# A four-layer graph network on one core: the residuals of layer 3's bf16 parts move from GpSimd to VectorE, one copy on ScalarE is dropped, and every engine's order is written anew

## The chip, the core and the metric

The program runs on one core of a Trainium2 chip. The metric is the device time of one execution in microseconds. Its five engines run queues of their own and meet at semaphores: TensorE (PE), VectorE (DVE), ScalarE (ACT), GpSimd (POOL) and SyncE (SP), which issues all DMAs.

## The reference

`x` and `adj` are 128 graphs of 128 nodes with 128 features. Four layers follow each other, each with a residual and a layer norm:

```python
x = layernorm(x + L0(x, adj, adj, ...))   # attention, 8 heads, edge bias, masked softmax, output projection
x = layernorm(x + L1(x, adj, ...))        # convolution of 17 taps, message passing with exp(-dist), gated unit
x = layernorm(x + L2(x, adj, ...))        # additive attention, softmax of e_i + f_j with mask
x = layernorm(x + L3(x, adj, ...))        # graph attention, 4 heads
# in L3:
e = e_i[:, :, :, None] + e_j[:, :, None, :]
e = where(e > 0, e, 0.2 * e); e = where(adj > 0, e, -9e15)
out = softmax(e) @ h
```

The change sits in L3's logits. Their sum `e_i + e_j` is a matmul of bf16 operands. Each fp32 number goes in as three bf16 parts: the rounded value, the rounded rest, and the rest of that.

## The kernel before, in words

Graphs go in 32 groups of four (`GB = 4`); a tile `[128, 512]` holds a group. All four layers of different groups are in flight together. Each engine has a function `step(t)` that lists its operations in an order written out by hand, each with the group it works on (`t - 38` and so on), and a loop runs it for all `t`. Operations whose group is out of range do nothing, so at the start only layer 0 runs and at the end only layer 3. The constant in `t - 38` matters only beside the others of the same engine: every engine runs its own stream.

PSUM has eight banks, `B[0]` to `B[7]`, and nearly every result of PE passes one. An operation that takes a bank first calls `freed(engine, s, users)`, which waits for the last live user in the list handed to it. So the order of an engine, the bank of each result and these lists belong together.

On PE (L839 to L976) the scores of layer 0 come in two halves (`scores`, L540), on slices of 32 rows of the array, `values` (L562), `targets` (L792), `values3` (L819) and `embed` (L664) on slices of 32 columns, `logits3` (L801) and `distances` (L683) again on rows. The rest uses the whole array. Helpers: every transposition is recorded at L508, the convolution's products at L605, the gates' matmuls at L708.

On DVE `seed_edges` (L1368) writes the edge bias into a bank before the scores add to it, and `seed_mask3` (L1603) does it for layer 3. `row_max` (L1382) and `row_max3` (L1611) take the negated row maxima, on which the exponentials on ACT, `exps` (L1011) and `exps3` (L1169), wait. ACT also copies nearly all banks to SBUF (`keep_...`), applies `leaky` (L1162), and makes the squares (L1069) that `sides` (L1440) on DVE needs for the distances. Copies of the transposed probabilities are L1028 (layer 0) and L1186 (layer 3). POOL takes the differences for the convolution (`fir_first`, L383, writes `xs`; `fir_second`, L397, writes `xd` and `xf`), multiplies `aT` by the mask (L413) and computes 1/sqrt by pow (L370).

The bf16 parts arise like this. `targets` puts e_i and e_j, repeated on several partitions, into the first 128 columns of `B[2]`. `keep_ej` (L1154) on ACT copies them to `ej` in fp32 (L1159) and to `ejh` in bf16 (L1160). `split_ej` (L415) on POOL subtracts: `ejt`, `ejv`, `ejd`, `eju`, `ejw` (L424 to L432), where a factor `neg_s` of 0 or -1 on each partition says which part this partition holds. Then four instructions L435 and one L436 make `ejm` and `eim`, the operands of `logits3`, by a factor and an addend on each partition.

SP (L305) loads the group's inputs: `xt` into two buffers, `xn` into two, `at` into three, `an` into six, and stores the result.

## Time and profile before

| what | value |
|---|---|
| median of 3 runs | 1408.46 us (1406.12 to 1408.89) |
| the profiled execution | 1408.24 us |
| its span, from the first instruction to the last | 1406.5 us |
| mean granted TensorE clock | 0.98 |
| PE, DVE, ACT, POOL busy | 96%, 86%, 84%, 42% |
| matmul instructions | 13330 |
| HBM traffic | 31 GB/s |

The span is the stretch that the profile's rows cover; the execution's own time has 1.7 us around it. A busy engine is one with an instruction under way: for PE, whose matmuls overlap, the record of a matmul reaches beyond the start of the next, so the starts tell more than the durations. In the tables a row ends with the idle time of the engine before it and what ended that.

### The profile page before, as it was taken

The numbers are of one execution on the slowest core, as the hardware profiler recorded it, in microseconds if no ns is written. First come the engines' busy times: TensorE is split into PE (matmuls) and PEld (weight loads), VectorE is DVE, ScalarE is ACT, GpSimd is POOL, SyncE is SP. The second block draws the span as 40 slices with busy tenths as digits, with TensorE's granted clock in tenths as the row PEclk, the third lists the DMA queues.
The fourth block names the chain that finished last, engine by engine and source line by source line (L and its number), as shares of the span: only waits on it lengthen the run. The fifth ranks groups of instructions, "written<-read, shape, count | busy, mean of one in ns | idle before, by whom it ended". The sixth has DMA issues, their size and how long they took to land.

```text
span 1406.5 us, 40636 instructions
## 1 busy us (share of the span) xinstructions
PE 1344.6 (96%) x13330; PEld 1043.0 (74%) x13330; DVE 1212.4 (86%) x3407; ACT 1185.0 (84%) x4450; POOL 596.5 (42%) x918
## 2 busy tenths in 40 slices
PE   6799999999999999999999999999999999999974
PEld 3577778877777877777787777787777778777753
DVE  7658889889999988999888999989898999888874
ACT  6877888988888998888898888889888888986664
POOL 1123444544344444435344434445443444545532
PEclk8999999999999999999999999999999999999995
DMA  3101010001011011101101101110110111000000
GB/s 134 31 31 32 31 32 31 17 32 39 16 40 39 25 38 39 32 24 39 39 24 39 40 17 38 39 39 24 39 39 17 39 39 32 24 17 31 9 16 24
DMA packets 23826, 46.88 MB, mean 33 GB/s; under 512 B 2753, under 2 KB 2754, under 8 KB 23490
## 3 DMA queue, kind: packets, MB, share of 16 engines
q1 hardware_dynamic: 23618, 44.27, 10.0%
q8 instruction: 110, 1.80, 0.5%
q14 instruction: 98, 0.80, 0.2%
HBM read 35.88 MB, written 8.39 MB: 31 GB/s over the span
## 4 chain that ended last, share of the span: by engine, by line
PE 89%; ACT 4%; DVE 4%; issue 2%; POOL 1%; DVEq 0%; POOLq 0%; ACTq 0%
PE B L708 18%; PE B L605 17%; PE B L508 14%; PE B L548 5%; PE B L572 4%; PE B L618 3%; PE B L519 2%; PE B L534 2%; PE B L761 2%; PE B L789 2%; PE B L662 2%; PE B L702 2%; PE B L827 2%; PE B L595 2%; PE B L773 2%; PE B L679 2%
## 5 line engine op out<-in xcount | busy, mean ns | idle before, releaser
L1019 ACT ACTIVATE e<-B,nm 128x128 f32<-128x128 f32 x1024 | 362.7, 384 | 12.8 <-DVE nm L1387 12.8
L508 PE MATMUL B<-ident,e 128*128 128x128 f32 x1536 | 233.5, 279 | 17.2 <-ACT pT L1028 8.8
L1377 DVE SCALAR_TENSOR_TENSOR B<-an,rowb,mask 128x512 f32<-128x512 f32 x256 | 190.6, 789 | 50.9 <-ACT h L1152 42.2
L1019 ACT ACTIVATION_READ_ACCUMULATOR e<-B,nm 128x1 f32 x1024 | 231.0, 226 | 0.0
L508 PEld LDWEIGHTS B<-ident,e 128*128 128x128 f32 x1536 | 178.8, 143 | 35.9 <-issue 12.3
L1177 ACT ACTIVATE e<-l,nm 128x128 f32<-128x128 f32 x512 | 198.7, 402 | 5.5 <-DVE nm L1616 5.5
L377 POOL TENSOR_TENSOR veps<-meanv,eps 128x4 f32<-128x4 f32 x128 | 26.4, 206 | 399.6 <-DVE meanv L1350 399.6
L1387 DVE TENSOR_REDUCE nm<-B 128x4 f32<-128x512 f32 x256 | 168.7, 673 | 26.2 <-PE B L548 26.0
L1028 ACT ACTIVATE pT<-B 128x512 f32<-128x512 f32 x256 | 155.6, 620 | 1.7 <-PE B L508 1.7
L380 POOL TENSOR_TENSOR rstd<-veps,neghalf 128x4 f32<-128x4 f32 x128 | 130.0, 1016 | 10.0
L391 POOL TENSOR_TENSOR xs<-xs 128x288 f32<-128x288 f32 x32 | 40.8, 1276 | 203.6 <-ACT xs L1059 203.6
L708 PE MATMUL B<-x1T,wm 128*128 128x512 f32 x192 | 102.4, 615 | 0.9 <-ACT nmT L1099 0.4
L1177 ACT ACTIVATION_READ_ACCUMULATOR e<-l,nm 128x1 f32 x512 | 103.0, 201 | 0.0
L548 PEld LDWEIGHTS B<-kh,qT 32*128 32x128 f32 x2048 | 63.8, 188 | 50.6 <-issue 47.9
L708 PE MATMUL B<-xcT,wm 128*128 128x512 f32 x192 | 98.2, 593 | 0.0
L708 PE MATMUL B<-nmT,wm 128*128 128x512 f32 x192 | 98.0, 592 | 0.0
L1115 ACT ACTIVATE tr<-B,gb 128x512 f32<-128x512 f32 x32 | 22.0, 687 | 88.0 <-PE B L708 88.0
L1616 DVE TENSOR_REDUCE nm<-l 128x4 f32<-128x512 f32 x128 | 86.9, 679 | 9.7 <-ACT l L1167 9.3
L605 PE MATMUL B<-xd,wm 128*128 128x128 f32 x640 | 90.5, 279 | 3.0 <-DVE B L1481 3.0
L1608 DVE TENSOR_SCALAR B<-an 128x512 f32<-128x512 f32 x128 | 81.8, 686 | 12.9 <-ACT pT L1028 12.9
L1167 ACT ACTIVATE l<-B 128x512 f32<-128x512 f32 x128 | 72.8, 594 | 23.2 <-PE B L809 22.1
L1186 ACT ACTIVATE pT<-B 128x512 f32<-128x512 f32 x128 | 76.8, 600 | 17.3 <-PE B L508 16.3
(200 smaller groups left out, 3423.5 us busy)
## 6 DMA issues: line engine op xcount, KB each, us to landing
xt<-in_x_t SPq DMA_DIRECT2D x32, 256.0 KB, 3.4
an<-in_adj_n SPq DMA_DIRECT2D x32, 256.0 KB, 2.9
xn<-in_x_n SPq DMA_DIRECT2D x32, 256.0 KB, 3.0
at<-in_adj_t SPq DMA_DIRECT2D x32, 256.0 KB, 2.7
out_x<-xo SPq DMA_DIRECT2D x32, 256.0 KB, 3.3
wm<-in_mats SPq DMA_DIRECT2D x1, 1088.0 KB, 9.1
wm<-in_mats SPq DMA_DIRECT2D x1, 832.0 KB, 6.7
wm<-in_mats SPq DMA_DIRECT2D x1, 320.0 KB, 2.9
```

The lines of the kernel that those rows point to most:

```text
L380: pool.tensor_tensor(rstd[i][:, :], veps[i][:, :], neghalf[:, :], ALU.pow)\
L508: last = mm(g(dst, b), g(src, b), ident[:, :], is_transpose=True, start=(b == 0), stop=True, skip_group_check=True)
L548: last = mm(g(banks[j], b), qT[r, b * N:(b + 1) * N], kh[r, e, b * N:(b + 1) * N], start=False, stop=True, skip_group_check=True)
L605: last = mm(phases(bank[:, :])[:, slot], w, src[:, :, c:c + Q], start=(start and c == 0), stop=True, skip_group_check=True)
L708: last = mm(bank[:, :], wm[:, w + j * N:w + (j + 1) * N], src[:, :], start=(n == 0 and not onto), stop=(n == len(parts) - 1), skip_group_c ...
L1019: last = fn(g(e0[:, h % 2, :], b), g(bank, b), ACT.Exp, bias=nm0[:, h % 4, b:b + 1], accum_out=sum0[s % 2][:, b, head(h):head(h) + 1])
L1028: fn(pT0[:, h, :], bank[:, :], ACT.Copy).then_inc(q["pT_ready"], 1)
L1177: last = fn(g(e3[:, b % 2, :], h), g(l3[:, b % 2, :], h), ACT.Exp, bias=nm3[:, b % 2, h:h + 1], accum_out=sum3[s % 2][:, b, h:h + 1])
L1377: v.scalar_tensor_tensor(out=bank[:, :], in0=an[s % AN][:, :], scalar=we[:, head(h):head(h) + 1], in1=mask0[:, :], op0=ALU.mult, op1=ALU.a ...
L1387: v.tensor_reduce(nm0[:, h % 4, :], per(bank[:, :]), AX, ALU.max, negate=True).then_inc(q["nm_ready"], 1)
L1608: v.tensor_scalar(per(bank[:, :]), g(an[s % AN], b).unsqueeze(1).broadcast_to([128, H3, N]), 0.0, NEG3, ALU.is_le, ALU.mult).then_inc(q["s ...
L1616: v.tensor_reduce(nm3[:, b % 2, :], per(l3[:, b % 2, :]), AX, ALU.max, negate=True)\
```

## The change

`keep_ej` makes one copy, `ejh`, and waits for the `ejw` of the group before. A new function `residuals3` on DVE makes `ejv`, `ejd` and `ejw` in three instructions, the first of which reads the bank itself. `split_ej` keeps the last five instructions. The prologue's bank for small products is `B[0]` in place of `B[5]`. The order on all five engines is new, and with it many banks and all lists for `freed`. Every engine but SP has its groups shifted by five more steps.

```diff
-ROWS, SMALL = 3, 5
+ROWS, SMALL = 3, 0
...
-STEPS = GROUPS + 46
+STEPS = GROUPS + 51
...
             def step(t):
+                store(t - 9)
+                load_xn(t - 2)
+                load_at(t - 4)
+                load_an(t)
                 load_xt(t)
-                load_at(t - 2)
-                load_an(t)
-                load_xn(t)
-                store(t - 10)
...
                 wait(pool, q["e3_ps"], GB * s)
-                pool.wait_ge(q["ej_ready"], s + 1)
-                pool.tensor_scalar(ejt[:, :], ejh[:, :], neg_s[:, 0:1], 1.0, ALU.mult, ALU.mult).then_inc(q["ej_t1"], 1)
-                pool.wait_ge(q["ej_t1"], s + 1)
-                pool.tensor_tensor(ejv[:, :], ejt[:, :], ej[:, :], ALU.add).then_inc(q["ej_v"], 1)
-                pool.wait_ge(q["ej_v"], s + 1)
-                pool.tensor_scalar(ejd[:, :], ejv[:, :], 1.0, 1.0, ALU.mult, ALU.mult).then_inc(q["ej_d"], 1)
-                pool.wait_ge(q["ej_d"], s + 1)
-                pool.tensor_scalar(eju[:, :], ejd[:, :], neg_s[:, 1:2], 1.0, ALU.mult, ALU.mult).then_inc(q["ej_t2"], 1)
-                pool.wait_ge(q["ej_t2"], s + 1)
-                pool.tensor_tensor(ejw[:, :], eju[:, :], ejv[:, :], ALU.add).then_inc(q["ej_w"], 1)
                 pool.wait_ge(q["ej_w"], s + 1)
...
-                rsqrt(1, t - 43)
-                rsqrt(3, t - 46)
...
+                rsqrt(3, t - 51)
+                rsqrt(1, t - 48)
...
             def keep_ej(s, bank):
...
-                wait(act, q["ej_split"], s)
+                wait(act, q["ej_w"], s)
                 act.wait_ge(q["ej_ps"], s + 1)
-                fn(ej[:, :], bank[:, 0:N], ACT.Copy)
                 fn(ejh[:, :], bank[:, 0:N], ACT.Copy).then_inc(q["ej_ready"], 1)
...
+            def residuals3(s, bank):
+
+                if not live(s):
+                    return
+                wait(dve, q["ej_split"], s)
+                dve.wait_ge(q["ej_ready"], s + 1)
+                v.scalar_tensor_tensor(out=ejv[:, :], in0=ejh[:, :], scalar=neg_s[:, 0:1], in1=bank[:, 0:N],
+                                       op0=ALU.mult, op1=ALU.add).then_inc(q["ej_v"], 1)
+                dve.wait_ge(q["ej_v"], s + 1)
+                v.tensor_copy(ejd[:, :], ejv[:, :]).then_inc(q["ej_d"], 1)
+                dve.wait_ge(q["ej_d"], s + 1)
+                v.scalar_tensor_tensor(out=ejw[:, :], in0=ejd[:, :], scalar=neg_s[:, 1:2], in1=ejv[:, :],
+                                       op0=ALU.mult, op1=ALU.add).then_inc(q["ej_w"], 1)
```

The new orders, from the added lines of the three long `step` functions (the lists for `freed` and some calls are left out; the removed lines are the orders of the kernel before). PE:

```diff
+                gate_r(t - 46, B[3], (("n3_done", -3, 1, 1), ("em_ready", 0, 1, 1), ("kh1_ready", 3, 1, 1),
...
+                scores(t - 43, 0, (B[6], B[4], B[1], B[2]))
+                gate_z(t - 46, B[0], (("r2_done", -1, 1, 1), ("pT3_ready", -2, 4, 1),
...
+                sums_T(t - 44, B[3], (("tr_ready", -2, 1, 1), ("n3_done", -5, 1, 1),
...
+                probs3_T(t - 48, 1, B[7], (("r2_done", 1, 1, 1), ("qT_ready", 5, 1, 1),
...
+                values(t - 44, 0, B[5], (("pT_ready", 0, 8, 8), ("em_ready", -2, 1, 1),
...
+                values(t - 44, 1, B[5], ())
+                gate_hn(t - 46, B[3], (("recT_ready", 2, 1, 1), ("tr_ready", 0, 1, 1),
...
+                probs_T(t - 43, 0, B[7], (("pT3_ready", -5, 4, 2), ("r2_done", -4, 1, 1),
...
+                x1_T(t - 45, B[4], (("exp_done", 2, 8, 2), ("l3_done", -3, 4, 4), ("exp_done", 1, 8, 7),
...
+                hidden3(t - 48, B[6], (("exp_done", 5, 8, 1), ("xc_ready", 2, 1, 1), ("l3_done", 0, 4, 2),
...
+                probs_T(t - 43, 1, B[5], (("oT_ready", -1, 1, 1), ("pT_ready", -1, 8, 8),
...
+                gate_in(t - 46, B[0])
+                project_v(t - 43, B[7], (("pT_ready", 0, 8, 1), ("pT3_ready", -5, 4, 2),
...
+                probs_T(t - 43, 2, B[1], (("exp_done", 0, 8, 3), ("ln_out1", -4, 1, 1),
...
+                scores(t - 43, 1, (B[3], B[6], B[4], B[5]))
+                conv1(t - 45, B[1], (("pT_ready", 2, 8, 3), ("exp_done", 2, 8, 3), ("ln_out1", -2, 1, 1),
...
+                x3_T(t - 47, B[2], (("exp_done", 4, 8, 4), ("nmT_ready", 1, 1, 1), ("em_ready", 1, 1, 1),
...
+                probs3_T(t - 48, 2, B[0], (("n_ready", 2, 1, 1), ("tz_ready", 2, 1, 1),
...
+                project_out(t - 44, B[7], (("v_ready", 1, 1, 1), ("pT_ready", 1, 8, 1),
...
+                probs3_T(t - 48, 3, B[1], (("hp_ready", 3, 1, 1), ("pT_ready", 5, 8, 3),
...
+                targets(t - 47, B[2], (("x3T_ready", 0, 1, 1), ("exp_done", 4, 8, 4),
...
+                probs_T(t - 43, 3, B[0], (("pT3_ready", -5, 4, 3), ("n_ready", -3, 1, 1),
...
+                values3(t - 48, B[7], (("res0_done", 4, 1, 1), ("v_ready", 5, 1, 1), ("pT_ready", 5, 8, 1),
...
+                embed(t - 45, B[1], (("pT3_ready", -3, 4, 4), ("hp_ready", 0, 1, 1), ("pT_ready", 2, 8, 3),
...
+                logits3(t - 47, (B[3], B[6], B[0], B[4]))
+                probs_T(t - 43, 6, B[2], (("pT_ready", 0, 8, 6), ("v0_done", -2, 1, 1), ("ej_v", -4, 1, 1),
...
+                project_k(t - 42, B[3], (("l3_done", -5, 4, 1), ("exp_done", -1, 8, 5),
...
+                hidden2(t - 46, (B[2], B[5]), (("pT_ready", 3, 8, 7), ("pT_ready", 3, 8, 6),
...
+                conv_own(t - 45, 0, B[6])
+                distances(t - 45, (B[7], B[5], B[2], B[3]), (("v2_done", 0, 1, 1), ("o3T_ready", -3, 1, 1),
...
+                conv_own(t - 45, 1, B[6])
+                out3_T(t - 48, B[3], (("em_ready", 3, 1, 1), ("kh1_ready", 6, 1, 1), ("l3_done", 1, 4, 1),
...
+                project_q(t - 42, B[7], (("em_ready", -3, 1, 1), ("v2_done", -3, 1, 1),
...
+                probs3_T(t - 47, 0, B[0], (("l3_done", 0, 4, 3), ("pT_ready", 4, 8, 5),
...
+                gather(t - 45, B[2], (("em_ready", 0, 1, 1), ("hb_done", -1, 1, 1), ("pT_ready", 2, 8, 7),
...
+                numerators(t - 46, (B[0], B[7]), (("pT3_ready", -1, 4, 1), ("l3_done", -1, 4, 3),
...
```

ACT:

```diff
+                exps3(t - 49, 2)
+                tanh_r(t - 47, B[3])
+                keep_probs(t - 45, 7, B[5])
+                exps(t - 44, 0, B[6])
+                exps(t - 44, 1, B[4])
+                keep_sums(t - 45, B[3])
+                tanh_z(t - 47, B[0])
+                keep_probs3(t - 49, 1, B[7])
+                exps3(t - 49, 3)
+                exps(t - 44, 2, B[1])
+                keep_h3(t - 49, B[6])
+                keep_x1(t - 46, B[4])
+                keep_probs(t - 44, 0, B[7])
+                keep_probs(t - 44, 1, B[5])
+                exps(t - 44, 3, B[2])
+                keep_probs(t - 44, 2, B[1])
+                tanh_n(t - 47, B[0])
+                keep_v(t - 44, B[7])
+                conv_input(t - 46, B[1])
+                keep_x3(t - 48, B[2])
+                keep_probs3(t - 49, 2, B[0])
+                keep_probs3(t - 49, 3, B[1])
+                keep_ej(t - 48, B[2])
+                exps(t - 44, 4, B[3])
+                keep_out3(t - 49, B[7])
+                keep_d(t - 46, B[1])
+                keep_probs(t - 44, 3, B[0])
+                exps(t - 44, 5, B[6])
+                squares(t - 46)
+                exps(t - 44, 6, B[4])
+                keep_probs(t - 44, 4, B[0])
+                keep_probs(t - 44, 5, B[2])
+                exps(t - 44, 7, B[5])
+                message_relu(t - 46)
+                leaky(t - 48, 0, B[3])
+                leaky(t - 48, 1, B[6])
+                keep_probs(t - 44, 6, B[2])
+                exps3(t - 48, 0)
+                keep_k(t - 43, 0, B[3])
+                keep_k(t - 43, 1, B[3])
+                exp_edges(t - 47)
+                leaky(t - 48, 2, B[0])
+                affinity(t - 46, (B[7], B[5], B[2], B[3]))
+                exps3(t - 48, 1)
+                conv_relu(t - 46, B[6])
+                keep_q(t - 43, B[7])
+                keep_probs3(t - 48, 0, B[0])
+                leaky(t - 48, 3, B[4])
+                keep_gathered(t - 46, B[2])
```

DVE:

```diff
+                seed_edges(t - 43, 2, B[1], (("ln_out1", -4, 1, 1), ("m1_done", -3, 1, 1),
...
+                row_scales(t - 47, (B[0], B[7]))
+                seed_edges(t - 43, 3, B[2], (("nmT_ready", -3, 1, 1), ("em_ready", -3, 1, 1),
...
+                residual2(t - 47, (B[0], B[7]))
+                invert_sums(t - 44)
+                stats2(t - 47)
+                row_max(t - 43, 0, B[6])
+                row_max(t - 43, 1, B[4])
+                norm0(t - 45)
+                half_tanh(t - 46)
+                aggr2(t - 47)
...
+                divide(t - 44, B[5])
+                reset_hn(t - 46, B[3], B[0], (("tz_ready", 0, 1, 1), ("r2_done", -1, 1, 1),
...
+                seed_edges(t - 43, 4, B[3], (("g1_done", -3, 1, 1), ("recT_ready", -1, 1, 1),
...
+                seed_edges(t - 43, 5, B[6], (("h3_ready", -5, 1, 1), ("exp_done", 0, 8, 1),
...
+                seed_edges(t - 43, 6, B[4], (("x1T_ready", -2, 1, 1), ("exp_done", 0, 8, 2),
...
+                seed_edges(t - 43, 7, B[5], (("pT_ready", 0, 8, 2), ("oT_ready", -1, 1, 1),
...
+                norm2(t - 47)
+                stats3(t - 49)
+                z_times_n(t - 46)
+                row_max(t - 43, 4, B[3])
+                aggr3(t - 49)
+                gru_out(t - 46)
+                row_max(t - 43, 5, B[6])
+                residual0(t - 44, B[7])
+                residuals3(t - 47, B[2])
+                stats0(t - 44)
+                row_max(t - 43, 6, B[4])
+                seed_mask3(t - 47, 0, B[3], (("exp_done", 4, 8, 5), ("g1_done", 1, 1, 1),
...
+                shared_to_all(t - 45, B[2])
+                sides(t - 45)
+                message_bias(t - 45, B[1])
+                seed_mask3(t - 47, 1, B[6], (("exp_done", 4, 8, 6), ("h3_ready", -1, 1, 1),
...
+                row_max(t - 43, 7, B[5])
+                seed_mask3(t - 47, 2, B[0], (("pT_ready", 4, 8, 5), ("pT_ready", 4, 8, 4),
...
+                seed_mask3(t - 47, 3, B[4], (("exp_done", 4, 8, 7), ("x1T_ready", 2, 1, 1),
...
+                stats1(t - 46, B[1])
+                shared_to_phases(t - 45, B[7])
+                aggr1(t - 46)
+                row_max3(t - 47, 0)
+                shared_to_halves(t - 45, B[7], B[6], (("l3_done", -2, 4, 2), ("exp_done", 2, 8, 6),
...
+                invert_sums3(t - 48)
+                row_max3(t - 47, 1)
+                hidden_bias(t - 46, (B[2], B[5]))
+                edge_mask(t - 42)
+                norm3(t - 49)
+                hidden_times_e(t - 46)
+                norm1(t - 46, B[1])
+                row_max3(t - 47, 2)
+                seed_edges(t - 42, 0, B[6], (("xc_ready", -3, 1, 1), ("l3_done", -5, 4, 2),
...
+                aggr0(t - 44)
+                divide3(t - 48, B[3])
+                seed_edges(t - 42, 1, B[4], (("l3_done", -5, 4, 4), ("exp_done", -1, 8, 7),
...
```

## Rows read from the trace of the kernel before

**Rows 1.** The page: busy time of each engine, and the chain that ended last.

```profile
PE 1344.6 (96%) x13330; PEld 1043.0 (74%) x13330; DVE 1212.4 (86%) x3407; ACT 1185.0 (84%) x4450; POOL 596.5 (42%) x918
...
PE 89%; ACT 4%; DVE 4%; issue 2%; POOL 1%; DVEq 0%; POOLq 0%; ACTq 0%
```

**Rows 2.** Windows: us, PE, PEld, DVE, ACT, POOL busy, PE clock, DMA share, GB/s.

```profile
397.90:1141.40 743.50, 740.18 (x7488) 578.67 (x7488) 673.41 (x1892) 662.22 (x2503) 335.51 (x504) 1.00 0.11 34
...
1330.00:1406.50 76.50, 45.38 (x328) 33.16 (x326) 48.74 (x166) 41.21 (x143) 23.30 (x42) 0.73 0.05 18
```

**Rows 3.** Waits of PE, 397.9 to 1141.4 us: total, times, longest.

```profile
PE B L519 <- ACT l L1167: 3.2, 18, 0.2
```

**Rows 4.** Timeline of PE: start, us, engine, line, op, out<-in.

```profile
700.22 1.17 PE L548 MATMUL B<-kh,qT 32*128 32x128 f32 x32
...
727.19 0.39 PE L809 MATMUL B<-ejm,eim 32*128 32x512 bf16 x4
...
732.20 0.50 PE L692 MATMUL B<-lr,ll 32*128 32x128 f32 x8
```

**Rows 5.** Timeline of ACT, the same period.

```profile
719.14 0.33 ACT L1160 ACTIVATE ejh<-B 128x128 bf16<-128x128 f32 x1
719.63 0.60 ACT L1193 ACTIVATE o3T<-B 128x512 f32<-128x512 f32 x1 [0.16 <-PE B L827]
...
722.60 0.53 ACT L1075 ACTIVATE sqr<-dd,sel 128x128 f32<-128x128 f32 x1
...
727.70 1.09 ACT L1167 ACTIVATE l<-B 128x512 f32<-128x512 f32 x2 [0.28 <-PE B L809]
...
729.57 1.27 ACT L992 ACTIVATE kh<-B,parity 128x512 f32<-128x512 f32 x2 [0.30 <-PE B L519]
```

**Rows 6.** Timeline of POOL, the same period.

```profile
715.83 1.37 POOL L391 TENSOR_TENSOR xs<-xs 128x288 f32<-128x288 f32 x1 [6.60 <-ACT xs L1059]
...
720.85 0.36 POOL L424 TENSOR_SCALAR ejt<-ejh,neg_s 128x128 f32<-128x128 bf16 x1
...
723.26 1.87 POOL L435 TENSOR_SCALAR ejm<-ejw,mid_t,mid_i 128x128 bf16<-128x128 f32 x4
...
733.90 1.28 POOL L413 TENSOR_TENSOR aT<-aT,at 128x512 f32<-128x512 f32 x1 [2.75 <-ACT aT L1089]
```

**Rows 7.** Single lines of code: duration ns min/median/max, first and last start us.

```profile
L1580 DVE SCALAR_TENSOR_TENSOR r<-B,wr,x x128: 340/341/351, 123.9 to 1367.8; 128x128 f32<-128x128 f32 x128
...
L1554 DVE COPY hg<-eg x32: 165/1257/1269, 117.5 to 1363.7; 128x8 f32<-128x8 f32 x32
...
L1446 DVE SCALAR_TENSOR_TENSOR lr<-dd,sel,sqr x32: 334/438/454, 73.0 to 1327.9; 128x128 f32<-128x128 f32 x32
...
L1377 DVE SCALAR_TENSOR_TENSOR B<-an,rowb,mask x256: 742/753/1115, 7.0 to 1250.4; 128x512 f32<-128x512 f32 x128
...
L405 POOL TENSOR_TENSOR xf<-xs x32: 1083/1534/1567, 70.6 to 1324.2; 128x420 f32<-128x420 f32 x32
...
L391 POOL TENSOR_TENSOR xs<-xs x32: 792/1377/1381, 67.8 to 1321.0; 128x288 f32<-128x288 f32 x32
```

**Rows 8.** Timeline of DVE, the same period.

```profile
715.87 0.67 DVE L1505 TENSOR_TENSOR zn<-zminus,nT 128x512 f32<-128x512 f32 x1
...
717.97 0.69 DVE L1412 TENSOR_TENSOR r<-B,xn 128x512 f32<-128x512 f32 x1 [0.82 <-PE B L595]
718.58 0.68 DVE L1387 TENSOR_REDUCE nm<-B 128x4 f32<-128x512 f32 x1
...
733.95 1.26 DVE L1554 COPY hg<-eg 128x8 f32<-128x8 f32 x1
```

**Rows 9.** The chain that ended last, 1340 us to the end: start, us, what.

```profile
1352.58 0.28 ACT ej L1159
...
1355.62 1.09 POOL ejm L435 x3
...
1389.80 2.08 PE B L789 x8
```

More of the change, by code:

```diff
@@ L483, in _ @@
             pe.wait_ge(q["flat_set"], 1)
-            for i in (0, 1, 2):
+            for i in (1, 2, 4):
                 set_bank(i)
@@ L1195, in step @@
             def step(t):
-                conv_relu(t - 42, B[6])
-                keep_probs3(t - 44, 0, B[5])
-                keep_q(t - 39, B[0])
-                leaky(t - 44, 3, B[4])
-                keep_gathered(t - 42, B[2])
-                keep_probs(t - 40, 7, B[5])
-                tanh_r(t - 42, B[3])
-                exps3(t - 44, 2)
-                exps(t - 39, 0, B[6])
-                exps(t - 39, 1, B[4])
-                tanh_z(t - 42, B[0])
-                keep_sums(t - 40, B[3])
@@ L1221, in step @@
-                keep_x3(t - 43, B[2])
-                keep_probs3(t - 44, 3, B[7])
-                exps(t - 39, 4, B[6])
-                keep_ej(t - 43, B[2])
-                keep_out3(t - 44, B[7])
-                keep_d(t - 41, B[1])
-                keep_probs(t - 39, 3, B[0])
-                exps(t - 39, 5, B[3])
-                squares(t - 41)
-                exps(t - 39, 6, B[4])
-                keep_probs(t - 39, 4, B[0])
-                keep_probs(t - 39, 5, B[2])
-                exps(t - 39, 7, B[5])
@@ L1234, in step @@
-                message_relu(t - 41)
-                leaky(t - 43, 0, B[3])
-                leaky(t - 43, 1, B[6])
-                keep_probs(t - 39, 6, B[2])
-                keep_k(t - 38, 1, B[3])
-                keep_k(t - 38, 0, B[3])
-                exps3(t - 43, 0)
-                leaky(t - 43, 2, B[0])
-                exp_edges(t - 42)
-                affinity(t - 41, (B[3], B[7], B[5], B[2]))
-                exps3(t - 43, 1)
+                exps3(t - 49, 2)
+                tanh_r(t - 47, B[3])
@@ L1699, in step @@
-                stats1(t - 41, B[1])
-                shared_to_phases(t - 40, B[7])
-                aggr1(t - 41)
-                row_max3(t - 42, 0)
-                shared_to_halves(t - 40, B[7], B[6], (("l3_done", -2, 4, 2), ("exp_done", 2, 8, 5),
-                    ("exp_done", 2, 8, 1), ("xc_ready", -1, 1, 1)))
-                stats0(t - 39)
-                hidden_bias(t - 41, (B[2], B[5]))
-                row_max3(t - 42, 1)
-                norm3(t - 44)
-                hidden_times_e(t - 41)
```

338 lines of the change are left out of this document (120 added, 218 removed).

## The prediction

> **What bounds the kernel now.** I read the page first: the matmul engine is busy 96% of the span, and is 89% of the chain that ended last [rows 1]. Then the stages: of PE's 13330 matmuls each of the 32 groups has 416, so the 7488 between 397.9 and 1141.4 us are 18 groups [rows 1, 2], in 743.5 us at full clock, so 41.3 us a group, with PE busy for 740.2 of it; the last 76.5 us have PE busy for 45.4 only, at clock 0.73 [rows 2]. In the steady stretch PE waits by the profile for one thing, 0.2 us a group, at L519 [rows 3]. So in the middle a change pays only if it takes PE's small stalls away, and costs if it makes new ones; at the end PE waits for chains through the other engines. One executed period, 700.22 (scores) to 741.61, serves as my ruler [rows 4]; all clock times below are in it.
>
> The profiled execution took 1408.24 us, 1.7 over its span; the median is 1408.46, so the two stand for each other. A measurement here tells about 0.2%, 2.8 us, from no change.
>
> **Part by part: edits with one answer.** The banks are renamed; the set-up loop still sets seven; each engine keeps its instructions but for those below. PE loses and gains nothing. It alternates between whole-array matmuls and those on row or column slices; values0 and values1 become one block, targets leaves values3, so there are seven such blocks a group as before, and adding up PE's starts I get the instruction behind them as far from the scores as in the ruler, within 0.02 us. 0 us. SP: store, xn, at, an, xt in place of xt, at, an, xn, store. What the first load now stands behind is the layer 3 mask seeding of six groups earlier (for an), about 727 in the ruler; xt, the last of the five, is wanted by a project_k a period later. 0 us. POOL's rsqrt order: norm 3's statistics are ready long before, 0 us. Bank B2 is released by the first residual instead of the copy, still before conv_both wants it: 0 us.
>
> **The copy dropped.** ACT issues two copies 0.16 us apart and the second stays, at 719.14. Next on ACT stands the copy of values3, for which it waited 0.16 us [rows 5], so the gain goes into that wait: 0 us. But keep_ej moves ahead of exps 4: ready at 718.46 rather than 719.47.
>
> **The residuals.** POOL loses five instructions, 0.36 + 0.46 + 0.30 + 0.37 + 0.45 us, which with their handovers take 720.85 to 723.26 [rows 6]. That is off the path in the middle: the five masks behind them take 2.3 more, to 725.55, and logits3 starts at 727.19 [rows 4]. DVE gains three dependent instructions. First: one SBUF, one PSUM operand, 128x128; the nearest row is L1580, 0.34 [rows 7]. Second, an SBUF copy to bf16: between the 0.17 of the 8-element copy L1554 and L1580's 0.34 [rows 7]; I take 0.2, since the copy has one operand only. Third, two SBUF operands: L1446 at its least, 0.33 [rows 7]. With 0.05 between them, 1.0 us in all.
>
> But such operands have another price beside POOL. The copy L1554 takes 0.165 at least and 1.257 in the median; in the timeline it starts at 733.95, 0.05 after POOL's mask product, and ends with it [rows 6 to 8]. The two-operand seed L1377 takes 0.753 in the median and 1.115 where it meets a POOL instruction [rows 7]. L1580, one operand in PSUM, never lengthens. In the new order DVE reaches the residuals at 718.5, while POOL runs fir_second: conv_input ends about 0.65 later than now (conv1 stands behind scores1), so xd runs about 718.6 to 719.7 and xf, 1.08 at its least [rows 7], behind it. So the second residual waits for xd, 0.65 us, and the third for xf: from 0.35 (the seed's excess) to 1.09 (the copy's excess) [rows 7]; I take the middle, 0.7. The residuals end near 720.85 instead of 719.5. Bounds: 1.0 us to 2.75 us in all.
>
> The Trainium skill, "SBUF — State Buffer", Who interferes with whom, says that VectorE and GpSimd share one port pair as an exclusive lock, held for the whole instruction by whoever issues first. By that sentence taken literally the third residual would wait out all of xf (0.9 more than unhindered), and the sum would be 1419.3 in place of 1413.9. The trace agrees on the waiting but not on who wins: z_times_n started 0.04 after POOL's xs and ran its normal 0.67, while xs took 1.37 instead of its least, 0.79 [rows 6 to 8].
>
> **What waits for them.** Behind the residuals DVE has stats0 (0.78), row_max 6, seed_mask 0, shared_to_all (0.60 each, as the starts are apart [rows 8]): 720.85 + 2.58 = 723.4. Next is sides, which waits for ACT's second square, 723.13 as now [rows 5]. So of the cost only what passes 720.6 counts: 0.2 us. From there the chain has no gap: sides 0.71, then message_bias, mask 1, row_max 7, masks 2 and 3, 0.60 each, the last 0.69: 727.2, plus 0.07 to PE, against 727.19 [rows 4]. **Term 1: logits3 late by 0.1.** Row_max 7 ends at 726.0, now 721.4; behind it ACT has exps 7 (1.37) and message_relu (0.5), so leaky 0 can start at 727.9 and not at 727.70 [rows 5], and project_k waits for leaky 0 [rows 3]: **term 2: 0.12 more.** On DVE stats1, shared_to_phases, aggr1 (1.83) come before row_max3 0, which so ends at 729.6. ACT now has exps3 0 (1.53) ahead of both keep_k (1.27 [rows 5]): they end at 732.48. The distances need B3 from the second keep_k; in the ruler they start at 732.20 [rows 4], with 0.22 of delay at 732.42. **Term 3: 0.12 with the handover.** Sum 0.34 us a group. Layer 3 runs together with layer 1 in 27 of the periods: **+9.2 us**.
>
> Now for what the new order spares. Gate_hn in B3, residual2 before the row maxima, exps3 2 before tanh_r, for which ACT stood idle: each fills a wait of an engine that isn't the bound, 0 us. The copy L1554 may now slip ahead of POOL's product and save DVE 1.09 us; after it nothing of PE's waits on DVE until the seeds, 0 us.
>
> **The end.** Twice, for groups 30 and 31, the residuals are on the chain: ej at 1352.58, ejm at 1355.62 [rows 9], 3.04 us, and the same again 23 us later. DVE is free and POOL idle there, so the three take 0.33 + 0.07 + 1.0 + 0.15 = 1.55: 1.45 saved, twice 2.9. At 1389.80 hidden3 has waited for the copy of pT3 [rows 9], since both use B3; in B6 it goes about 2 us earlier, then transposition 3 waits for exps3 3 near 1391.3: 0.9 saved. At the start, scores1 waits for keep_probs 1 (seed 7 uses its bank) and exps 4 comes some 0.1 later in three groups: +0.3. **-3.5 us**.
>
> Sum: 1408.24 + 9.2 - 3.5 = **1413.9 us**, 0.4% slower. Own range of this case 1411.5 to 1418.
>
> **Rivals.** (a) Faster: POOL does not hold DVE up, or the residuals end before 720.6. For: DVE stands 0.8 us idle at residual0 [rows 8], so there is slack. Then terms 1 and 2 vanish, and if row_max3 0 ends by 729.3 also term 3: 1408.24 - 3.5 = 1404.7. Chance 0.23. (b) No change: the residuals hide, but keep_k behind exps3 0 does not: 0.14 a group (row_max3 0 ends at 729.45 at best by my chain), 27 x 0.14 = 3.8, 1408.5. Chance 0.20. (c) Slower still: the third residual waits for the whole of xf, 0.2 more; terms 0.29, 0.12, 0.13, together 0.54: 1404.7 + 14.6 = 1419.3. The port rule of the Trainium skill gives this one. It decides from 720.6 on; every 0.1 us later costs 2.7 us. Against: xs above. Chance 0.20. (d) That SP's new order starves a load: excluded by the slack above, under 0.01.
>
> The forecast has 0.37. So slower 0.57, same 0.20, faster 0.23. Range 1403 to 1424: below, case (a) with its small stalls; above, (c) with 0.17 a group more, as my sums along queues may be off by 0.2.
>
> **What would show it.** The new copy near 0.8 us instead of 0.2 and the last residual near 1.0 instead of 0.34 in the middle, both short in the last two groups; PE waits at logits3 and the distances that rows 3 do not have; a period of 41.6 to 41.7 us; project_k's wait longer; the last 76 us shorter by 3. It is wrong if the period stays at 41.3 or less, or if sides still has DVE waiting for the squares.

## The result, and the profile after

| | before | after |
|---|---|---|
| median | 1408.89 us (7 runs, 1406.12 to 1411.19) | 1413.09 us (7 runs, 1412.05 to 1414.99) |
| the profiled execution, its span | 1408.24, 1406.5 | 1413.09, 1411.4 |

The ratio is 1.0032, 95% interval 1.0022 to 1.0042: 0.3% slower, where 1413.9 was forecast. The total came out closer than its parts did, which is luck, as the account of the parts below shows.

The page after: busy time of each engine, and the chain that ended last.

```profile
PE 1348.3 (96%) x13330; PEld 1048.3 (74%) x13330; DVE 1238.0 (88%) x3503; ACT 1182.6 (84%) x4418; POOL 509.0 (36%) x758
...
PE 69%; DVE 14%; ACT 10%; issue 5%; POOL 1%; DVEq 0%; ACTq 0%; POOLq 0%
```

Beside [rows 1]: POOL is busy for 87.5 us less and DVE for 26 more, 0.8 us for each of the 32 groups. That is less than the residuals take (2.2 us a group in the middle, below), above all because the copy L1538 (L1554 before) has become short, 0.164 us in the median instead of 1.257. ACT has 32 copies fewer. The bound is PE as before, but the chain now runs over DVE and ACT for 24% instead of 8% of the span.

Windows: us, PE, PEld, DVE, ACT, POOL busy, PE clock, DMA share, GB/s.

```profile
397.90:1141.40 743.50, 736.96 (x7456) 577.33 (x7455) 683.87 (x1937) 658.08 (x2468) 279.45 (x408) 1.00 0.11 34
1330.00:1411.40 81.40, 51.69 (x422) 39.63 (x422) 57.68 (x185) 43.72 (x148) 24.79 (x41) 0.79 0.05 17
```

The same 743.5 us hold 32 matmuls fewer than in [rows 2], and PE is busy for 3.2 us less. From project_k to project_k, over 18 groups, the period is 41.514 us against 41.306 before.

Waits of PE after, 397.9 to 1141.4 us: total, times, longest.

```profile
PE B L506 <- ACT l L1151: 4.4, 18, 0.5
PE B L679 <- issue: 1.0, 4, 0.2
```

The first is project_k's wait of [rows 3], 1.2 us more. The second is at the distances, and small only because most of that wait lies under the modelled length of the matmul before. PE's starts tell more. I added up the steps from each start to the next over the 18 groups, by what follows what. Mean per group, after less before: from the convolution to the distances +0.171 (0.384 against 0.214); around y_T +0.060 (nothing before); from the transposition to project_k +0.067; from gather to the embedding behind it -0.08; the rest -0.01. Sum +0.21.

The timelines show the new residuals and what stands around them. DVE, then POOL, ACT and PE of one period after: start, us, engine, line, op, out<-in, [idle before <- what ended it].

```profile
765.30 0.35 DVE L1593 SCALAR_TENSOR_TENSOR ejv<-ejh,neg_s,B 128x128 f32<-128x128 bf16 x1 [0.57 <-ACT ejh L1144]
765.68 0.84 DVE L1596 CAST ejd<-ejv 128x128 bf16<-128x128 f32 x1
766.57 1.07 DVE L1598 SCALAR_TENSOR_TENSOR ejw<-ejd,neg_s,ejv 128x128 f32<-128x128 bf16 x1
...
769.52 0.68 DVE L1442 TENSOR_TENSOR vT<-B,x1T 128x512 f32<-128x512 f32 x1
770.13 0.35 DVE L1430 SCALAR_TENSOR_TENSOR lr<-dd,sel,sqr 128x128 f32<-128x128 f32 x1
770.40 0.35 DVE L1432 SCALAR_TENSOR_TENSOR ll<-dd,sel,sql 128x128 f32<-128x128 f32 x1
770.66 0.68 DVE L1421 TENSOR_TENSOR msg<-B,rowb 128x512 f32<-128x512 f32 x1
```

```profile
765.33 1.11 POOL L401 TENSOR_TENSOR xd<-xs 128x432 f32<-128x432 f32 x1
766.41 1.08 POOL L402 TENSOR_TENSOR xf<-xs 128x420 f32<-128x420 f32 x1
767.82 1.75 POOL L422 TENSOR_SCALAR ejm<-ejw,mid_t,mid_i 128x128 bf16<-128x128 f32 x4 [0.33 <-DVE ejw L1598]
```

```profile
769.43 0.57 ACT L1060 ACTIVATE sqr<-dd,sel 128x128 f32<-128x128 f32 x1
```

```profile
771.44 0.62 PE L495 MATMUL B<-ident,yT 128*128 128x128 f32 x4
...
774.00 0.39 PE L796 MATMUL B<-ejm,eim 32*128 32x512 bf16 x4
```

The first residual is short beside POOL's xd. The second ends 0.08 us after xd, the third 0.15 after xf. They take 2.3 us where 1.0 would do. But sides (L1430) starts 0.13 us behind ACT's square, so most of that was hidden.

How closely the two arrive is told by the start of sides beside the end of shared_to_all (L1442) ahead of it: where nothing holds DVE up, the next instruction starts before the recorded end of the last (sides 0.09 us before it in the kernel before, in the median of the 18 groups), here 0.01 behind it. So DVE stood about 0.1 us for the squares. Behind sides stands message_bias (L1421, ends at 771.34), and 0.10 later PE starts y_T, which waits for it.

So there are two accounts of the slower middle: the stretch of the residuals (the forecast), or the orders, namely a chain without slack through ACT's squares to y_T, and exps3 0 ahead of keep_k. The experiments are to tell them apart.

Periods in them are means over 18 groups from PE's starts. The ratios are to the kernel before, run beside each of the three sets (medians 1410.10, 1408.79 and 1408.84 us). The changed kernel was timed with the result only, so differences from its 1413.09 us compare different sets, and those of a microsecond or two rest on the periods and not on the times.

### The profile page after: what moved, and what is told of

Same layout as the page of the kernel before. It is cut to its first block, busy times and chain, and to the rows that moved or that the text cites. A ratio compares the mean times of both kernels' runs of the same rounds, so it can differ in the third digit from the quotient of the medians.

```text
span 1411.4 us, 40570 instructions
## 1 busy us (share of the span) xinstructions
PE 1348.3 (96%) x13330; PEld 1048.3 (74%) x13330; DVE 1238.0 (88%) x3503; ACT 1182.6 (84%) x4418; POOL 509.0 (36%) x758
## 4 chain that ended last, share of the span: by engine, by line
PE 69%; DVE 14%; ACT 10%; issue 5%; POOL 1%; DVEq 0%; ACTq 0%; POOLq 0%
PE B L695 18%; PE B L495 11%; PE B L592 10%; PE B L535 5%; ACT e L1004 5%; PE B L559 4%; DVE nm L1371 3%; DVE B L1606 3%; PE B L506 2%; PE B L649 2%; PE B L760 2%; PE B L521 2%; PE B L748 2%; PE B L689 2%; PE B L513 2%
## 5 line engine op out<-in xcount | busy, mean ns | idle before, releaser
L1004 ACT ACTIVATE e<-B,nm 128x128 f32<-128x128 f32 x1024 | 367.8, 398 | 46.5 <-DVE nm L1371 39.6
L495 PE MATMUL B<-ident,e 128*128 128x128 f32 x1536 | 241.1, 281 | 21.8 <-ACT pT L1013 6.5
L1004 ACT ACTIVATION_READ_ACCUMULATOR e<-B,nm 128x1 f32 x1024 | 242.8, 237 | 0.0
L495 PEld LDWEIGHTS B<-ident,e 128*128 128x128 f32 x1536 | 183.2, 144 | 72.0 <-issue 50.0
L374 POOL TENSOR_TENSOR veps<-meanv,eps 128x4 f32<-128x4 f32 x128 | 34.9, 272 | 342.7 <-DVE meanv L1334 342.7
L1013 ACT ACTIVATE pT<-B 128x512 f32<-128x512 f32 x256 | 151.9, 632 | 3.0 <-PE B L495 2.2
L388 POOL TENSOR_TENSOR xs<-xs 128x288 f32<-128x288 f32 x32 | 30.9, 965 | 231.5 <-ACT xs L1044 231.5
L1161 ACT ACTIVATION_READ_ACCUMULATOR e<-l,nm 128x1 f32 x512 | 109.5, 214 | 0.0
L1170 ACT ACTIVATE pT<-B 128x512 f32<-128x512 f32 x128 | 77.5, 607 | 15.9 <-PE B L495 15.8
L410 POOL TENSOR_TENSOR aT<-aT,at 128x512 f32<-128x512 f32 x32 | 40.8, 1276 | 127.3 <-ACT aT L1074 127.3
L592 PEld LDWEIGHTS B<-xd,wm 128*128 128x128 f32 x640 | 78.8, 189 | 8.0 <-issue 4.1
```

The source lines that it names most:

```text
L495: last = mm(g(dst, b), g(src, b), ident[:, :], is_transpose=True, start=(b == 0), stop=True, skip_group_check=True)
L592: last = mm(phases(bank[:, :])[:, slot], w, src[:, :, c:c + Q], start=(start and c == 0), stop=True, skip_group_check=True)
L1004: last = fn(g(e0[:, h % 2, :], b), g(bank, b), ACT.Exp, bias=nm0[:, h % 4, b:b + 1], accum_out=sum0[s % 2][:, b, head(h):head(h) + 1])
L1013: fn(pT0[:, h, :], bank[:, :], ACT.Copy).then_inc(q["pT_ready"], 1)
L1161: last = fn(g(e3[:, b % 2, :], h), g(l3[:, b % 2, :], h), ACT.Exp, bias=nm3[:, b % 2, h:h + 1], accum_out=sum3[s % 2][:, b, h:h + 1])
```

## The experiments

**1. Four kernels: the residuals back, keep_k back, the residuals moved, the residuals alone.** a_pool takes the residual part of the change back in the new orders:

```diff
+                fn(ej[:, :], bank[:, 0:N], ACT.Copy)
                 fn(ejh[:, :], bank[:, 0:N], ACT.Copy).then_inc(q["ej_ready"], 1)
...
-                residuals3(t - 47, B[2])
```

> The changed kernel with the residuals back on GpSimd and both copies back on ScalarE; all other orders as changed. Theory 1 (the forecast: the stretched residuals on VectorE are what delays logits3, project_k and the distances): VectorE loses 2.2 us a group, the period falls from 41.51 to about 41.30 us, 27 x 0.21 = -5.7 us, and the end loses the 1.45 us of the last group: about 1409 us. Theory 2 (the stretch hides, because `sides` behind it waits for ScalarE's squares anyway; the distances wait because exps3 0 now stands ahead of keep_k): nothing is gained in the middle, and the second copy puts the squares up to 0.16 us later: period 41.5 to 41.7 us, 1414.5 to 1419 us.

Measured: 1422.26 us, 1.0088 (1.0074 to 1.0102), period 41.752. That is above both theories. Taking the residuals off DVE made the kernel slower by 9 us and not faster by 4, which speaks against their stretch as the main cost; but the second copy came back with them, and a_copy below separates the two. PE waits 0.17 us more at y_T and 0.10 more behind gather. The period's 0.238 us make some 6 of the 9 us (27 x 0.238); group 6 started 2.1 us later than in the changed kernel's profile.

a_keepk:

```diff
-                exps3(t - 48, 0)
                 keep_k(t - 43, 0, B[3])
                 keep_k(t - 43, 1, B[3])
+                exps3(t - 48, 0)
```

> The changed kernel with keep_k 0 and 1 ahead of exps3 0 on ScalarE, as before the change; nothing else. Theory 2 (queue order on ScalarE): the two copies end 1.5 us earlier, PE's step from convolution to distances falls from 0.38 to about 0.21 us, the period from 41.51 to 41.34, 27 x 0.17 = -4.6: 1408.5 us. Rival: exps3 0 ends 1.25 us later, and the transposition of its result or leaky 2 behind it holds PE up instead: 1412 us or more.

Measured: 1408.62 us, 0.9991 (0.9982 to 1.0000), 4.5 us less than the changed kernel. The period is 41.319, and PE's step to the distances 0.213 us, as before the change. ACT's timeline after, where the copies (L977) stand behind four exps3 without a gap and end at 737.54, and PE's, which starts the distances 1.13 us after the convolution's last block:

```profile
734.74 0.40 ACT L1161 ACTIVATE e<-l,nm 128x128 f32<-128x128 f32 x1
...
736.30 1.24 ACT L977 ACTIVATE kh<-B,parity 128x512 f32<-128x512 f32 x2
```

```profile
736.66 1.05 PE L592 MATMUL B<-xf,wm 128*128 128x128 f32 x8
737.79 0.45 PE L679 MATMUL B<-lr,ll 32*128 32x128 f32 x5
```

and the same two places in a_keepk, 0.98 us from the one to the other:

```profile
734.49 1.26 ACT L977 ACTIVATE kh<-B,parity 128x512 f32<-128x512 f32 x2 [0.30 <-PE B L506]
```

```profile
736.13 1.05 PE L592 MATMUL B<-xf,wm 128*128 128x128 f32 x8
737.11 0.50 PE L679 MATMUL B<-lr,ll 32*128 32x128 f32 x8
```

a_split cuts residuals3 in two (the first instruction stays) and calls the rest later on DVE:

```diff
                 seed_mask3(t - 47, 0, B[3], (("exp_done", 4, 8, 5), ("g1_done", 1, 1, 1),
...
+                residuals3_rest(t - 47)
                 shared_to_all(t - 45, B[2])
```

> The changed kernel with the second and third residual moved on VectorE behind stats0, row_max 6 and seed_mask 0, where GpSimd has finished xf; the first stays. Both theories expect them to take 0.23 and 0.35 us instead of 0.76 and 1.07. Theory 1 (the stretch is the cost): -0.2 us a group or a little more, 1407 to 1408 us. Theory 2 (`sides` waits for the squares anyway and starts at most 0.1 us earlier): 0 to -2 us, 1411 to 1413 us.

Measured: 1417.19 us, 1.0046 (1.0033 to 1.0059), period 41.594. Both theories missed: it is 4 us slower than the changed kernel. The period accounts for 2.2 of them (27 x 0.080); in the profile group 6 started 2.5 us later (196.5 instead of 194.0), which is within what starts of the same instructions differ by (below). The residuals are short, but DVE gains nothing by it:

```profile
770.96 0.22 DVE L1600 CAST ejd<-ejv 128x128 bf16<-128x128 f32 x1
771.21 0.35 DVE L1602 SCALAR_TENSOR_TENSOR ejw<-ejd,neg_s,ejv 128x128 f32<-128x128 bf16 x1
...
773.54 0.51 DVE L1430 SCALAR_TENSOR_TENSOR lr<-dd,sel,sqr 128x128 f32<-128x128 f32 x1 [1.38 <-ACT sqr L1060]
```

DVE stands idle for 1.38 us until the squares: the whole stretch was hidden there. And sides now meets POOL's ejm and eim (771.74 to 773.91), which puts 0.14 us on lr (0.509 in the median instead of 0.370); PE's step at y_T grew by 0.11. So the same wait came back in the one place that has no slack.

b_dve is the kernel before with this alone:

```diff
-                fn(ej[:, :], bank[:, 0:N], ACT.Copy)
...
                 row_max(t - 38, 7, B[5])
+                residuals3(t - 42, B[2])
```

> The kernel before with one part of the change alone: one copy on ScalarE, and the three residuals on VectorE, put behind row_max 7, where GpSimd has finished xf. All orders stay as before. Both theories: the residuals are short (0.35, 0.23, 0.35 us), the 1.0 us is taken up by VectorE's idle time ahead of the third mask, the period stays at 41.30, and the end is 1.45 us shorter once or twice: 1405.5 to 1407.5 us against 1408.9. Rival (a busy VectorE passes 1 us on): 0.3 to 0.5 us a group, 1416 to 1420 us.

Measured: 1495.44 us, 1.0605 (1.0591 to 1.0620), period 44.359. That is 88 us above what both theories expected, for a reason that neither had. Waits of PE in b_dve, 397.9 to 1141.4 us:

```profile
PE B L608 <- DVE ejv L1598: 34.2, 17, 2.8
```

The first residual reads bank 2 and so frees it, and conv_both behind it on PE waits for it, 2 us a group. The period grew by 3.05. The third microsecond lies behind the wait: in the period of the ruler PE stands idle for 1.96 us up to 721.48, and its granted clock, 1.00 before, is 0.76 from 721.5 to 723.5 and 0.50 (the lower of its two levels, 1.2 GHz) from 723.5 to 725.5 us, where the eight matmuls of message take 1.92 us. Behind row_max 7 is too late for the first residual: here the bank sets how late it can stand.

**2. Four more: the y_T chain, the start, the residuals alone again, the port.** a_swap:

```diff
+                message_bias(t - 45, B[1])
                 sides(t - 45)
-                message_bias(t - 45, B[1])
```

> The changed kernel with message_bias ahead of sides on VectorE; nothing else. From the four runs before: y_T (transposition of layer 2's input, bank 1) waits for message_bias, and that stands behind sides, which waits for ScalarE's squares. Theory 2 (this chain, not the stretched residuals, is VectorE's part of the price): PE's step before y_T falls by the 0.06 us that it has too much, the rest of VectorE's queue ends when it did, 41.51 to 41.45 us, 27 x 0.06 = -1.6: 1411.5 us. Theory 1 (the residuals' stretch): with nothing waiting for the squares, VectorE's whole queue is a chain from the residuals to row_max 7, and the distances' wait stays: 0 to -0.5 us.

Measured: 1409.82 us, 1.0006 (0.9997 to 1.0015), period 41.398. The 0.060 us at y_T are gone, with 0.030 at the distances and 0.022 at project_k: 0.117 us a group, twice what was expected, and 3.3 us less than the changed kernel, for one line.

a_fill:

```diff
+FIRST = 4
...
-                project_v(t - 43, B[7], (("pT_ready", 0, 8, 1), ("pT3_ready", -5, 4, 2),
...
+                if t - 43 >= FIRST:
+                    project_v(t - 43, B[7], (("pT_ready", 0, 8, 1), ("pT3_ready", -5, 4, 2),
...
                 scores(t - 43, 1, (B[3], B[6], B[4], B[5]))
+                if t - 43 < FIRST:
+                    project_v(t - 43, B[7], (("pT_ready", 0, 8, 1), ("pT3_ready", -5, 4, 2),
```

> The changed kernel in which PE issues project_v of the first four groups behind scores 1, as the kernel before does, and of all others where the change put it. Theory: PE's 2.1 us of project_v at half clock ahead of scores 1 of group 0 are what made the start 2.2 to 2.5 us longer: project_k of group 1 starts at 28.2 to 29 instead of 30.4 us, and the time falls by 2 us: 1411 us. Rival: the start is set by ScalarE's exponentials and VectorE's preparation, and the order on PE matters for group 0 alone or not: 0 to -0.5 us.

Measured: 1433.88 us, 1.0179 (1.0162 to 1.0196). The kernel was not what its expectation says: `FIRST` is set again further down in it, to 640 (`FIRST, SECOND = N * 5, WC2`), so project_v stood behind scores 1 for all groups, and the test of the start is spoilt for the total. What it shows: in the middle scores 1 then wait for DVE's seeds, which project_v had covered (period 42.035, 0.59 us a group at that step). At the start scores 1 came 1.9 us earlier (19.4 instead of 21.3 us), but project_k of group 1 still began at 30.8 us (30.4 in the changed kernel), so this place alone does not explain the longer start.

b_dve2 is b_dve with keep_ej ahead of exps 4, the first residual behind residual0 and the other two behind row_max 7:

```diff
+                keep_ej(t - 43, B[2])
                 exps(t - 39, 4, B[6])
-                keep_ej(t - 43, B[2])
...
                 residual0(t - 39, B[1])
+                residuals3(t - 42, B[2])
...
                 row_max(t - 38, 7, B[5])
+                residuals3_rest(t - 42)
```

> The kernel before with keep_ej (one copy) ahead of exps 4, the first residual behind residual0 on VectorE, so that bank 2 is free at 719.6 in the ruler and the convolution, 719.7, does not wait as it did in b_dve, and the other two behind row_max 7. All other orders as before. Theory 2: period 41.30 to 41.35 and the end 1.45 to 2.9 us shorter: 1406 to 1408.5 us against 1409. Rival: the first residual, which waits for the copy with VectorE's queue behind it, holds row_max 5 and the convolution up by 0.1 to 0.3 us a group: 1412 to 1417 us.

Measured: 1416.97 us, 1.0057 (1.0045 to 1.0070), period 41.658: the rival's number. It names the wrong place, though: PE now waits for keep_d (dd), which stands behind keep_ej and exps 4 on ACT. PE's step into the products of message, which wait for keep_d, is 0.474 us instead of 0.111.

```profile
PE B L669 <- ACT dd L1057: 3.4, 17, 0.2
```

So neither of the two places tried in the old order is free.

a_psum, where the lists for bank 2 also name `ej_d` in place of `ej_v`:

```diff
-                v.tensor_copy(ejd[:, :], ejv[:, :]).then_inc(q["ej_d"], 1)
+                v.scalar_tensor_tensor(out=ejd[:, :], in0=bank[:, 0:N], scalar=0.0, in1=ejv[:, :],
+                                       op0=ALU.mult, op1=ALU.add).then_inc(q["ej_d"], 1)
```

> The changed kernel in which the second residual, instead of a copy from SBUF, is bank times 0 plus ejv, so that one of its operands lies in PSUM (the result is the same number). If an operation with a PSUM operand never waits for GpSimd, it takes 0.35 us instead of 0.76, and the third, 0.4 us earlier, either gets in between xd and xf and is short (0.6 us) or waits for the end of xf (1.4 to 1.5 us instead of 1.07). Time by theory 2 the same within 0.5 us, as VectorE waits for the squares; by theory 1 -0.2 us a group if it gets in, the same if not.

Measured: 1413.06 us, 1.0027 (1.0015 to 1.0039), period 41.464: the residuals take 1.31 us instead of 2.34 in the periods shown, so they end 1.0 us earlier, and the time is the same. DVE now stands 1.06 us in front of sides (median), until the squares; of the stretch only 0.05 us a group had reached PE, at the distances and at y_T. DVE, then POOL of a_psum:

```profile
765.03 0.29 DVE L1596 SCALAR_TENSOR_TENSOR ejd<-B,ejv 128x128 bf16<-128x128 f32 x1
765.35 0.61 DVE L1599 SCALAR_TENSOR_TENSOR ejw<-ejd,neg_s,ejv 128x128 f32<-128x128 bf16 x1
```

```profile
764.68 1.13 POOL L401 TENSOR_TENSOR xd<-xs 128x432 f32<-128x432 f32 x1
765.75 1.16 POOL L402 TENSOR_TENSOR xf<-xs 128x420 f32<-128x420 f32 x1
```

With a PSUM operand the second takes 0.29 us beside a running xd. The third waits for the end of xd and gets in ahead of xf.

**3. The last four: the copy by itself, both repairs, both with the short residual, the end by itself.** a_copy only puts the dropped copy back (its result is read by nobody):

```diff
+                fn(ej[:, :], bank[:, 0:N], ACT.Copy)
                 fn(ejh[:, :], bank[:, 0:N], ACT.Copy).then_inc(q["ej_ready"], 1)
```

> The changed kernel with the dropped fp32 copy put back on ScalarE ahead of the other, its result read by nobody; the residuals stay on VectorE. Theory 2 (in the new order a chain without slack runs from keep_ej over the squares, sides and message_bias to PE's y_T): the squares come 0.16 us later and PE waits 0.15 us more before y_T and some at the embedding, as in the run with the residuals on GpSimd: period 41.51 to about 41.70, +4 to +6 us: 1417 to 1419 us. Rival (that run's loss came from GpSimd's five instructions; the copy goes into ScalarE's idle time, as the prediction had it): 1413 to 1414 us.

Measured: 1420.98 us (1417.80 to 1422.80), 1.0080 (1.0064 to 1.0096). The profiled execution took 1417.80, and its period is 41.709: +0.195 a group, at y_T (+0.124) and behind gather (+0.10 in all), less 0.03 at project_k. So of a_pool's 0.238 the copy makes 0.195, and the residuals' move to POOL 0.04: taking the stretched residuals off DVE brings nothing, with the copy in place. The median lies 3 us above the profiled execution: in three of the six the time stands 3.1 to 3.2 us over the span instead of 1.7, and the spans themselves reach from 1416.1 to 1419.7. Why they do is open.

a_both is a_keepk and a_swap together.

> The changed kernel with keep_k ahead of exps3 0 on ScalarE and message_bias ahead of sides on VectorE. If the two add up as their waits do (0.19 us at the distances, and 0.06 to 0.08 us at y_T and project_k): period 41.24 to 41.27 us, 1406.5 to 1407.5 us, 0.1 to 0.2% under the kernel before. Rival: the two act on one chain and the second adds nothing: 1408.5 us.

Measured: 1406.04 us, 0.9978 (0.9968 to 0.9988), period 41.258. It beats both kernels: 7 us under the changed one, 0.2% under the one before, with all residuals on DVE. The two repairs add up, as expected.

a_both_psum adds a_psum's edit.

> The same with the second residual reading a PSUM operand (bank times 0 plus ejv), so that the residuals end 0.9 us earlier. Theory 1's last chance: now that nothing on VectorE waits for the squares, row_max 7 comes up to 0.9 us earlier, exps 7 and leaky 0 with it, and PE's step to project_k falls from 0.50 to its least, 0.45 us: 0.05 x 27 = -1.4 us against the run without it. Theory 2: ScalarE is busy without a gap up to there, so 0 to -0.5 us.

Measured: 1406.17 us, 0.9977 (0.9968 to 0.9987), period 41.231. Project_k's step fell by 0.026 us; the time cannot tell it.

b_tail is the kernel before, with the residuals of the last two groups on DVE:

```diff
+                if s < TAIL:
+                    pool.wait_ge(q["ej_ready"], s + 1)
...
+                if not live(s) or s < TAIL:
+                    return
```

> The kernel before, with the residuals of groups 30 and 31 alone on VectorE (behind row_max 7) and one copy for these; all other groups and all orders as before. The prediction's term for the end, 1.45 us for each of the two groups: -2.9 us, 1406 us. Rival, from the chain of the changed kernel, where only group 31's gain reached the end: -1.45 us, 1407.5 us. Nothing if VectorE's queue holds the residuals up there: 1409 us.

Measured: 1407.76 us, 0.9988 (0.9978 to 0.9997), 1.1 us less by the medians. The interval, 0.4 to 3.1 us less, holds both the prediction's 2.9 and the rival's 1.45, so the trace has to decide. In it targets 30 to targets 31 take 21.06 us instead of 22.61, and targets 31 to logits3 31 4.50 instead of 6.09: 1.55 and 1.59 less. Both groups gain, as the prediction had it. (Of the 1.59 some 0.2 lie ahead of the copy, where targets ran at granted clock 1.00.) Its start was 3.1 us longer than in the profile before, with the same instructions. The granted clock was 0.90 in both in the first 34 us, and lower after that; windows of the kernel before, then of b_tail:

```profile
34.00:77.00 43.00, 34.69 (x426) 27.96 (x427) 26.00 (x51) 35.96 (x157) 6.26 (x9) 0.92 0.16 50
```

```profile
34.00:77.00 43.00, 34.06 (x398) 26.19 (x399) 27.01 (x53) 33.28 (x145) 6.27 (x9) 0.84 0.15 48
```

## Why the prediction was right, point by point

**The residuals' cost on DVE** was right in mechanism and size. Forecast: 0.65 us waiting for xd, 0.7 for xf, end at 720.85 of the ruler. Measured in the middle: the second 0.757 against 0.216 alone, so 0.54; the third 1.071 against 0.351, so 0.72. In the period shown it ends 6.36 us ahead of logits3, which is 720.83 in the ruler; in the median of the 18 groups 6.47, which is 720.72. The 0.7 was the middle of a range and not a mechanism: what happens is what rival (c) says, the third waits until xf has ended, and it is 0.72 and not 0.9 because it starts 0.16 us behind xf's start. Single lines after: ns min/median/max, first and last start.

```profile
L1596 DVE CAST ejd<-ejv x32: 226/756/1164, 143.9 to 1384.7; 128x128 bf16<-128x128 f32 x32
...
L1598 DVE SCALAR_TENSOR_TENSOR ejw<-ejd,neg_s,ejv x32: 351/1071/1198, 144.1 to 1385.0; 128x128 f32<-128x128 bf16 x32
```

**Terms 1 and 2, what the stretch costs**, rest on the step that failed. The forecast let DVE arrive at sides at 723.4, 0.27 us behind the squares at 723.13, and from there had a late chain to logits3 and project_k. The squares came as forecast: in the median they end 4.02 us ahead of logits3, which is 723.17. But wherever sides waits for them it starts 0.13 us behind their end, a handover that the forecast left out, so 723.3; and DVE was there at 723.2, since the residuals ended 0.13 us earlier than forecast and what stands behind them took 2.5 us and not 2.58. So it was DVE that waited, about 0.1 us. Sides then took 0.53 us, not 0.71, and DVE's last mask ended 0.27 us ahead of logits3. Term 1 (logits3 0.1 late) was 0: PE's step to logits3 is 0.205 us in both kernels. Term 2 (0.12 at project_k) was 0.067, of which the stretch has at most 0.03 (a_both against a_both_psum). All in all, shortening the residuals by 1.0 us saved 0.05 us a group (a_psum), where terms 1 to 3 had laid most of 0.34 at their door. Rival (b), that the residuals hide and keep_k does not, was the truer account, though it gave 1408.5: its 0.14 a group at the distances (0.171 measured) lacked y_T, project_k and the start.

**The signs** that the prediction named came in part. Came: the long second and third residual, both short in the last two groups (0.23 and 0.35 us), waits at the distances and a longer one at project_k, an end shorter by 3. Did not come: the wait at logits3, and the period of 41.6 to 41.7 (41.51). And one of its two signs of being wrong came: DVE still waits for the squares in front of sides, by 0.1 us. By its own sign, then, the forecast had the path through DVE wrong, and the total does not show it.

**Term 3, the distances behind exps3 0**, was right in its mechanism and too small: 0.12 forecast, 0.171 measured, and all of it went when keep_k went back.

**"The copy dropped: 0 us"** was wrong for the new order. I had read its slack in the order before, where ACT waited 0.16 us behind it [rows 5]. After the change ACT has no such gap up to the squares, and from there sides and message_bias lead to y_T. Put back, the copy costs 0.195 us a group. What the forecast had not priced at all is the other side of the same chain: message_bias behind sides, 0.060 us a group at y_T.

**The middle in sum**: 0.34 forecast, 0.21 measured. From project_k 6 to 31 the changed kernel lost 5.0 us, and 0.4 more up to targets 30.

**The start**: +0.3 forecast. In the two profiles project_k of group 1 starts at 28.0 and 30.4 us, of group 6 at 191.4 and 194.0: 2.6 us. Part of it differs between executions of the same instructions: the three traces besides that have the start of the kernel before begin group 1 at 29.2 (b_tail, b_dve) and 30.5 (b_dve2), and b_tail has group 6 at 194.5. The nine that have the changed start, a_fill left out, begin group 1 at 30.4 to 31.6 and group 6 at 193.6 to 196.5. So the order has a share, 1.8 us at group 1 between the two means. At the same granted clock (0.90 in the first 34 us, 0.84 from there to 77), b_tail has 29.2 and 194.5, a_both_psum 31.5 and 196.1. The 2.6 us of the two profiles are thus part order, part chance of the execution; which place in the order makes its share stays open, since a_fill did not test it as meant.

**The end**: -3.8 forecast (-2.9 and -0.9), and the profiles give -3.2 from targets 30 on (54.5 and 51.3 us). Group 31's residuals gave 1.43 (1.45 forecast). Group 30's gave 1.3 up to its logits3 (4.59 us from targets, before 5.88), and that was lost again behind it: to the next targets it took 18.5 us instead of 16.7, so 23.07 in all against 22.61, where b_tail shows 1.55 less. The changed kernel's PE was granted 0.50 in the second half of that stretch (the lower of its two levels, 1.2 GHz, throughout), the kernel before 0.72 and b_tail 0.66 with 16.6 us, a_swap 0.63 with 17.2; so part is the clock, and the rest open. From logits3 31 to the end it takes 23.5 us instead of 25.8. a_swap at clock 0.65 takes 23.0 and b_tail, which has hidden3 in the old bank, 24.5 at 0.64, so the new order there, with hidden3 in bank 6, is worth 1.5 us, not 0.9; that the bank alone does it was not tested. The chain that ended last, first before [rows 9], now after:

```profile
1383.95 0.29 ACT ejh L1144
...
1384.33 0.36 DVE ejv L1593
...
1384.71 0.24 DVE ejd L1596
...
1384.97 0.35 DVE ejw L1598
1385.32 2.39 DVE B L1606 x4
1387.71 0.11 issue
1387.82 0.64 PE B L796 x4
```

From the copy to logits3 it is 3.87 us; between stand the three residuals and the four masks that DVE seeds behind them.

**Sum**: +2.6, +5.4, -3.2 = +4.8 between the profiled executions (4.85 measured), +4.2 between the medians. The forecast had +0.3, +9.2, -3.8. The middle was too dear by 3.8 us and the start too cheap by 2.3, which nearly cancelled; that the total came within 0.8 us is luck, the more so as the start differs by about as much between executions of the same instructions. The rival (c) was right about the port and wrong about the time. "SBUF — State Buffer", Who interferes with whom, in the Trainium skill has the shared port pair held for a whole instruction. The trace agrees (the third residual ends 0.15 us after xf), but the squares hid it.

## What to carry to other kernels

The slack of an instruction belongs to an order: when a change rewrites the order, read the slack of each dropped or added piece again along the new queues, up to the next wait of the bound engine. A stretched instruction costs only what passes the next wait behind it on its engine; ask what that wait is for before pricing the stretch. And with five queues and shared banks a place in a queue has two sides, what it waits for and what it frees: here one line up or down was worth 3 to 5 us, and how late the residuals could stand was set by the bank that the first one frees.

## What was not expected of the hardware

- The wait of a DVE instruction for a running POOL instruction depends on its operands: the same value computed with one PSUM operand took 0.29 us in every group where the copy from SBUF took 0.757 in the median (0.216 alone), both beside xd. The third residual, the same kind of instruction as the short one but with two SBUF operands, does wait. The Trainium skill, "SBUF — State Buffer", Who interferes with whom, says that DVE with at most one SBUF input outside its two-port modes does not contend; the trace agrees.
- DVE can get in between two POOL instructions that stand back to back: in a_psum the third residual ends 0.2 us after xf's recorded start, in 29 of the 30 groups where they meet, and xf takes 1.14 us instead of 1.09 in the median.
- The start differs between executions of the same instructions. In the four traces with the start of the kernel before, the granted clock of the first 34 us is 0.90, 0.90, 0.90 and 0.72, and group 1 begins at 28.0, 29.2, 29.2 and 30.5 us. At the same 0.90, the kernel before and b_tail still have group 6 3.1 us apart, with 0.92 and 0.84 granted from 34 to 77 us.
- A wait of PE can cost more than it lasts: in b_dve the wait of 2 us came with 1 us more behind it, in matmuls at the granted clock 0.50.
